# A context ring inside the last key/value head, and Wo loaded under the end of attention

## What is computed

```
def _L0_xattn_ref(latents, context, Wq, Wk, Wv, Wo, q_norm_w, k_norm_w):
    kv = jnp.concatenate([context, latents], axis=1)          # 1857 rows per batch
    q, k, v = latents @ Wq, kv @ Wk, kv @ Wv                  # 32 query heads, 8 key/value heads, 128 wide
    q, k = rms_norm(q, q_norm_w), rms_norm(k, k_norm_w)
    probs = softmax(q @ k.T / sqrt(128)) ; out = probs @ v
    return out @ Wo
x = x + tanh(g_xattn[0]) * _L0_xattn_ref(_layernorm(x), ctx_4096, Wq, Wk, Wv, Wo, q_norm_w, k_norm_w)
x = x + tanh(g_ffn[0]) * _L0_ffn_ref(_layernorm(x), c1_w, c2_w, w1, w2t)   # one row of each 32 chosen
```

## Time and profile before

| | |
|---|---|
| median of 3 runs | 3181.91 us (3180.02 to 3183.23) |
| the profiled execution | 3184.63 us, its span 3182.8 us, mean granted TensorE clock 0.962 |
| busy, share of the span | TensorE 93%, VectorE 78%, ScalarE 64%, GpSimd 44% |
| `prepare` | to about 242 us |
| `attend` | to about 2671 us |
| `project` | its matmuls from 2704 to 2910 us |
| `ffn` | to the end |

### The profile page before, as it was taken

One profiled execution on the slowest core, in us unless ns is written; L12 is line 12 of the kernel. 1 busy time (PEld: TensorE's weight loads), 2 busy tenths in 40 slices (PEclk: granted clock), 3 DMA queues, 4 the chain that ended last, 5 costly groups with the idle time before them and its releaser, 6 DMA issues. The chain is left out here.

```text
span 3182.8 us, 50915 instructions
## 1 busy us (share of the span) xinstructions
PE 2958.6 (93%) x14138; PEld 2398.5 (75%) x14138; DVE 2480.4 (78%) x3285; ACT 2045.6 (64%) x2899; POOL 1386.7 (44%) x791
## 2 busy tenths in 40 slices
PE   7996999999799999997999999899999993887899
PEld 6774888888578888875788888678888872775677
DVE  7773888888858888895888888958888895534765
ACT  3442787888758888884788788758888883211211
POOL 2330455566526655554455656526655554000000
PEclk9997999999999999998999999999999996998899
DMA  7873111121211112122111121211112112856200
GB/s 253 277 217 108 38 39 37 38 41 37 75 38 29 44 37 39 33 60 59 37 34 43 33 34 45 78 37 29 44 36 40 33 24 81 255 159 187 84 30 20
DMA packets 251492, 227.79 MB, mean 72 GB/s; under 512 B 45780, under 2 KB 193236, under 8 KB 250344
## 3 DMA queue, kind: packets, MB, share of 16 engines
q1 hardware_dynamic: 246600, 213.19, 24.5%
q0 software_dynamic: 2176, 8.39, 0.7%
q10 hardware_dynamic: 2592, 4.72, 0.5%
HBM read 156.92 MB, written 69.34 MB: 71 GB/s over the span
## 5 line engine op out<-in xcount | busy, mean ns | idle before, releaser
L877 POOL TENSOR_TENSOR att_sm<-att_sm,att_sc 128x1024 f32<-128x1024 f32 (+1 forms) x384 | 853.8, 2224 | 596.3 <-DVE att_pr L833 594.9
L691 PE MATMUL att_ppv<-att_pr,att_V 128*128 128x512 f32 (+1 forms) x2880 | 866.8, 411 | 27.6 <-DVE att_pr L833 27.1
L671 PE MATMUL att_pqk<-att_q,att_kT 128*128 128x512 f32 (+1 forms) x2880 | 835.5, 400 | 11.3 <-ACT att_sc L760 10.9
L632 PE MATMUL att_pkv<-att_ctxT,att_wkv 128*128 128x512 f32 (+1 forms) x3072 | 761.5, 378 | 5.1 <-DVE att_ctxT L807 4.8
L760 ACT ACTIVATE att_sc<-att_pqk,att_rk 128x512 f32<-128x512 f32 (+1 forms) x960 | 661.6, 690 | 157.0 <-PE att_pqk L671 134.5
L833 DVE TENSOR_TENSOR att_pr<-att_sc,att_pr 128x1024 fp32r<-128x1024 f32 (+1 forms) x512 | 642.0, 1254 | 34.4 <-ACT att_pr L771 21.3
L632 PEld LDWEIGHTS att_pkv<-att_ctxT,att_wkv 128*128 128x128 f32 x3072 | 562.4, 190 | 125.1 <-issue 5.3
L691 PEld LDWEIGHTS att_ppv<-att_pr,att_V 128*128 128x128 f32 (+1 forms) x2880 | 529.3, 193 | 146.5 <-DVE att_pr L833 40.7
L671 PEld LDWEIGHTS att_pqk<-att_q,att_kT 128*128 128x128 f32 (+1 forms) x2880 | 520.5, 185 | 140.3 <-ACT att_sc L760 20.6
L827 DVE TENSOR_TENSOR att_sc<-att_sc,att_pmax 128x1024 f32<-128x1024 f32 (+1 forms) x512 | 585.0, 1142 | 46.0 <-PE att_pmax L640 44.9
L771 ACT CAST att_pr<-att_sc 128x1024 fp32r<-128x1024 f32 (+1 forms) x512 | 511.4, 999 | 109.8 <-PE att_ppv L691 101.6
(11 more groups left out here) (129 smaller groups left out, 2620.3 us busy)
## 6 DMA issues: line engine op xcount, KB each, us to landing
q_scr<-pre_qT SPq DMA_DIRECT2D x128, 256.0 KB, 3.6
att_wkv<-kv_scr SPq DMA_DIRECT2D x64, 512.0 KB, 4.2
att_q<-q_scr SPq DMA_DIRECT2D x64, 512.0 KB, 4.1
o_scr<-att_oraw SPq DMA_DIRECT2D x64, 256.0 KB, 2.0
out_oraw<-o_scr SPq DMA_DIRECT2D x64, 256.0 KB, 4.8
out_rdb<-rd_scr SPq DMA_DIRECT2D x64, 256.0 KB, 5.1
att_sc<-in_ctx SPq DMA_DIRECT2D x16, 768.0 KB, 7.2
pre_wq_raw<-in_L_xattn_Wq SPq DMA_DIRECT2D x8, 1024.0 KB, 6.8
```

The lines of the kernel that those rows point to most:

```text
L632: mm = pe.matmul(bank, wkv[:, which, wp, t], ctxT[:, xp, t, a:z], start=(i == 0), stop=(i == len(terms) - 1))
L671: mm = pe.matmul(pqk[0:m, (h * NT + t) % 2], kT[:, kp, t * P:t * P + m], q[:, qp, h], start=(i == 0), stop=(i == 2))
L691: mm = pe.matmul(ppv[:], V[0:m, vp, t], pr[0:m, pp, (t // 2) % NP, t % 2], start=(t == 0 and i == 0), stop=(t == NT - 1 and i == 2))
L877: pool.tensor_tensor(sm[0:m, 0:w], sm[0:m, 0:w], sc[0:m, h, i:i + w], ALU.add).then_inc(sum_ok, w)
```

## The change

It has two parts and a new table.

**The ring.** The context rows no longer go into `sc`. A buffer `xr` has four slots of one tile each, loaded one tile at a time from ScalarE's DMA queue. The 13 tiles and the load of the latents are placed in the last head's own round (`LAST_SWAP`), each as soon as the V projection of the old batch has read its columns of `ctxT`; the next head's early steps are in that round too. `BOUNDARY` and `FIRST` between batches are gone: the first head of a batch runs the `MIDDLE` list. The tiles use the bank `pred`, which the transposes "mt" and "dt" use as well, so that every user of that bank waits for the one before it. At the very start (`START`) the tiles ("xt0") use three banks.

**The handover.** `handover` gives the two stages shared semaphores and buffers that lie on `ctxT`, on the ring and on the first half's scores. All 8 chunks of Wo (1 MB each) are loaded from SyncE's queue in the last round, after the last V chunk ("ldwo"). The first four units' outputs and three units' inverse sums are loaded in `TAIL` ("ldo"), after the last store of the output. `project` is rewritten with a placed order of its own: units flow from batch to batch, four buffers for the inverse sums instead of two, and each unit's load waits for the low part of the unit four before it.

**The table.** `TILE`, `END`, `CHUNK` and `LOADS` have new values.

```diff
+def handover(nc, ctx, d, Wo):
+    with ExitStack() as first:
+        sb = tools(nc, first, "share")[0]
+        heads = sb("wo", [P, 2 * KT * KVP])
+        tail = sb("wo_tail", [P, WC, D])
+        scores = sb("o_rd", [P, NT * 512])
...
+        ctxT = sb("ctxT", [P, 2, KT, KVP], F32R)
+        xr = sb("xr", [P, XS, D])
+        sc = [sb("sc0", [P, NT, HALF]), sb("sc1", [P, NT, HALF])]
...
-        TILE = dict(copy=0.29, pv=24.4, sub=19.5, exp=21.0, hi=21.6, lo=22.3, sum=23.6, max=1.18)
+        TILE = dict(copy=0.19, pv=24.4, sub=19.4, exp=21.0, hi=21.6, lo=22.4, sum=25.2, max=0.98)
...
-                   dt=(24.37, 24.37),
+                   dt=(23.67, 24.07),
...
-                 dict(k=(0.1, 0.34, 0.62), v=(20.0, 22.44, 22.62), khi=0.64, klo=0.57, kn=4.23, var=4.74, pow=7.34, vhi=21.84, vt=23.7, vthi=23.06, vtlo=22.84))
+                 dict(k=(-0.26, 0.0, 0.32), v=(22.3, 22.84, 22.92), khi=0.24, klo=0.47, kn=3.94, var=6.74, pow=12.84, vhi=21.64, vt=23.6, vthi=23.16, vtlo=23.44))
...
+        for i in range(CT):
+            at = max(at + 1.15, FREE[(S + min(i * P + P, L) - 1) // 512])
+            at = next((z + 0.7 for a, z in HELD if a - 1.1 < at < z + 0.7), at)
+            context += [(at, "xt", 0, i), (at + 0.3, "xhi", 0, i), (at + 0.6, "xlo", 0, i)]
+            ring += [(context[3 * (i - XS)][0] + 0.4 if i >= XS else -0.5 + 0.1 * i, "ldx", 0, i)]
...
+        swap = context + [(max(FREE[0], 0.1), "ldlat", 0, 0)] + ring
...
-        BOUNDARY = window((-1, -UT, late), (0, -UT, in_boundary), (0, 0, context), (0, UT - 3.33, start_early))
-        TAIL = window((-1, -UT, late))
+        handed = [(max(CHUNK[NC - 1]["v"]) + 0.5 + 0.01 * i, "ldwo", 0, i) for i in range(d["HEADS"] // WC)]
+        LAST_ONE = window((-1, -UT, late), (0, 0, own), (0, 0, handed))
+        LAST_SWAP = window((-1, -UT, late), (0, 0, own), (0, 0, swap), (1, UT, early))
+        TAIL = window((-1, -UT, late), (-1, -UT, [(NT + TILE["sum"] + NT - 0.7 + 0.01 * i, "ldo", 0, i) for i in range(SL)]))
...
+        BANK.update({(what, i): 2 for what, n in (("xt", CT), ("mt", NH), ("dt", NH)) for i in range(n)})
...
+            run(0, START, [], xb=0, fresh=0)
+            run(0, FIRST, [(0, START)], xb=0, fresh=0)
+            with eng.Fori(0, B - 1) as b:
+                with eng.Fori(1, KVH - 1) as r:
+                    run(b * KVH + r, MIDDLE, [(1, MIDDLE)], head=r)
+                run(b * KVH + (KVH - 1), LAST_SWAP, [(1, MIDDLE)], xb=b + 1, head=-1, fresh=1)
+                run(b * KVH + KVH, MIDDLE, [(1, LAST_SWAP)], xb=b + 1, fresh=0)
...
+                    if what == "ldx":
+                        act.wait_ge(xt_ps, AHEAD + xb * CT + max(t + 1 - XS, 0))
...
+                        act.dma_start(xr[0:w, t % XS], ctx_4096[bass.ds(xb, 1), t * P:t * P + w]
...
+        steps = [(v - 2.0, "mul", v) for v in range(NV)] + [(v - 1.6, "hi", v) for v in range(NV)]
+        steps += [(v - 1.3, "lo", v) for v in range(NV)] + [(v, "mm", v) for v in range(NV)]
+        steps += [(v - 4.1, "load", v) for v in range(NV)] + [(1.6 + t, "x", t) for t in range(BT)]
...
+        first = [(2 * (c // 2) + (-2.5, -1.5)[c % 2] + 0.8 * (c > 1), "whi", c) for c in range(NW)]
+        first += [(2 * (c // 2) + (-1.9, -1.2)[c % 2] + 0.8 * (c > 1), "wlo", c) for c in range(NW)]
```

More of the change, by code:

```diff
@@ L55, in program @@
     prepare(nc, dims, scratch, x, Wq, Wk, Wv, q_norm_w, k_norm_w)
-    attend(nc, dims, scratch, ctx_4096)
-    project(nc, dims, scratch, x, Wo, g_xattn)
+    with ExitStack() as ctx:
+        shared = handover(nc, ctx, dims, Wo)
+        attend(nc, dims, scratch, ctx_4096, shared)
+        project(nc, dims, scratch, x, g_xattn, shared)
     ffn(nc, dims, scratch, g_ffn, c1_w, c2_w, w1, w2t, out)
@@ L518, in rounds, with run @@
         def rounds(eng, step):
[L520 to L522 removed]
+            def run(n, steps_of, earlier, xb=None, head=0, fresh=None):
+                seen = [(dn - back, *u) for back, w in earlier for dn, *u in uses(w)]
                 for dn, what, h, t in steps_of:
[L524 to L528 removed]
@@ L530, in batch @@
-            def batch(b, loads_of_next):
-                n = b * KVH
-                run(n, FIRST, [(0, BOUNDARY)], xb=b, fresh=True)
+                    if user(what, h, t):
+                        step(n + dn, what, h, t, before=bank_before(seen, *user(what, h, t)), dn=dn, xb=xb, fresh=fresh)
+                        seen.append((dn, *user(what, h, t)))
+                    else:
+                        step(n + dn, what, h, t, xb=xb, dn=dn, head=head)
+            run(0, START, [], xb=0, fresh=0)
@@ L545, in grouped @@
+            run(B * KVH, TAIL, [(1, LAST_ONE)])
+        handed_sems = shared["o_in"] + shared["x_in"] + shared["x2_out"]
+        handed_sems += [shared[n] for n in ("whi_ok", "wlo_ok", "on_ok", "ohi_ok", "olo_ok", "o_ps", "x2_ok")]
         def grouped(n, h, g):
@@ L580, in _, with step @@
             def _(sp):
-                def step(n, what, h, t, before=None, dn=0, last=False, xb=None, head=0, fresh=False):
+                def step(n, what, h, t, before=None, dn=0, xb=None, head=0, fresh=None):
                     if what in ("ldwk", "ldwv"):
@@ L695, in step @@
                         pe.wait_ge(fold_ok, AHEAD + u + 1)
[L696 to L699 removed]
+                        wait_for_bank(n, dn, before, xb)
                         for c in range(4):
```

362 lines of the change are left out of this document (185 added, 177 removed).

## The result

The changed kernel takes **3078.93 us** (median of 4 runs, 3078.22 to 3080.34) against 3182.08 for the one before (4 runs, 3180.02 to 3183.23): ratio 0.9677, 95% interval 0.966 to 0.9694. That is 103 us faster, where 136 were forecast, and 4 us above the range. Its profiled execution took 3079.33 us, with a span of 3077.2 and a mean granted clock of 0.977. So 30.2 us are to be found between the forecast's sum of 3049.1 and 3079.3.

The account below looks back on a forecast made before the run. TensorE's work was taken to bound ordinary rounds (69.7 us), with 122.3 us lost between batches. The sum 3184.6 - 90 - 43.5 - 4 + 2 = 3049.1, with the runs' median 2.7 lower, gave 3046 us; range 3026 to 3075.

Parts of the forecast that it names:

- the swap rounds: The rounds at a batch boundary that hold the context tiles: forecast as one round of 80.4 us, 10.7 extra each boundary.
- first reduction: VectorE's first reduction of a head's first half, after the kernel's start: forecast 4 us sooner.
- start: Kernel's beginning: four single tiles first in their own queue, transposed some 5 us sooner; -4 us in all (-9 to +3).
- The table: Ordinary rounds of attention: new order can't go below 69.7 us, only get waits; +2 us over 28 rounds (-1 to +10).
- dt: Transposes on TensorE that wait for the fold in an ordinary round: taken as the tightest wait, slack 0.8 us.
- Ordinary rounds stall: Rival: slack at "dt" and the shared bank fails, TensorE waits 0.5 us each half; 28 us, 3074; chance 0.1.
- The ring: Last head's round at batch boundaries: 13 tiles add 5.7 us work and 5 us stall; gain 90 us (69 to 105).
- Between batches: Attention's batch boundaries: 43.3, 43.1 and 35.9 us lost, together 122.3, mostly waiting and slow clock.
- no stretch of low clock: Sign of being right: a boundary round of 75 to 88 us with TensorE's clock never low.
- The handover: Attention to `project`: TensorE starts at about 2685 instead of 2704.18, `project` ends at 2866.5; -43.5 us (36 to 50).
- Wo hides: End of attention: Wo's 8 MB, issued some 50 us earlier, are landed by then; the opposite rival, 3065, had chance 0.08.
- Locked out: Rival: in boundary rounds VectorE's low parts meet GpSimd's sums, 1.3 us more each, VectorE needs 89 us; 3073; chance 0.1.

Follow-up runs that it names:

- the late loads: Changed kernel, but with Wo and project's first inputs loaded by SyncE at the start of project, in one queue: 3106.02 us, 0.9769 of the kernel before.

## Why the prediction was wrong, step by step

Forecast and profiled execution differ by 30.2 us. Term by term, us against the forecast:

| step | forecast | measured | difference |
|---|---|---|---|
| ordinary rounds: wait for the copy | +2 in all | 31 waits, 20.6 | +18.6 |
| ordinary rounds: TensorE's own work | 69.67 | 70.45 - 0.67 = 69.78, 28 times | +3 |
| jump of the batch loop | 0 | 4.9 and 4.0 over a round of 70.45 | +8.9 |
| the swap rounds | 3 x 10.7 | 3 x (4.1 + 4.0) | -7.7 |
| first reduction | -4 | 322.38 to 320.40, -2 | +2 |
| last reciprocal to first matmul | 13.9 | 24.3 | +10.4 |
| `project`'s matmuls, with the slow start | 181.5 | 179.0 | -2.5 |
| `ffn` | 272.9 | 270.5 | -2.4 |

They add to 30.3. In `project` three matmuls take 0.69 us once the clock is full, and the forecast took 0.70. The last row is noise: `ffn` is between 270 and 274 us in all these profiles. The first reduction too comes anywhere from 315 to 321 us in kernels with the same start, so that of the **start** no more can be said than that it lost nothing: the first tile is transposed at 256.11 and not at 263.10, 7 us sooner where 5 were forecast, but only 2 of them are left at the first reduction.

- **The table** is the step that failed. "It can only get waits. The tightest one is 'dt'" looked at one wait and its slack. That one held, with more room than the 0.8 us worked out: the fold ended at 578.61 and TensorE's four transposes start without a wait at 581.72. The copy of the output, whose place had hardly moved (23.6 to 23.8), was no candidate, because TensorE had waited for it only once before, 0.2 us. What changed was the cover on TensorE: the matmuls between two products. The end of +10 that I gave this term was no bound at all.
- **The rival "Ordinary rounds stall"** had the size (28 us) and the sign, but at "dt" and the shared bank. Its chance was 0.1, and the run with the table alone has the wait without the shared bank.
- **The ring** was right, and better than forecast. The tiles' work is 73.17 + 72.82 - 2 x 69.74 = 6.5 us a boundary (5.7 forecast), and TensorE's waits for the tiles' low parts are 1.7 us where I took 5. No low clock in either swap round.
- **Between batches** the forecast had no term for the way back of the loop: it took all 122.3 us between batches as lost to the old order, and gave none of it to the jump. What it cost is 8.9 us, in two rounds, with the low clock behind it. So "no stretch of low clock" was right in the swap rounds and wrong in the round after. The rows of before held a sign of it: two boundaries lost 43 us and the last one, which no jump back follows, 35.9. Right after the first two, ScalarE stops twice without a wait that the trace names (2.5 and 5.5 us, then 2.4 and 5.8), and TensorE waits 4.2 and 4.6 us for it; after the third the largest such stop is 0.9. The kernel before at the first:

```profile
906.42 1.27 ACT L760 ACTIVATE att_sc<-att_pqk,att_rk 128x512 f32<-128x512 f32 x2 [5.47 <-issue]
```
```profile
907.16 1.65 PE L671 MATMUL att_pqk<-att_q,att_kT 128*128 128x512 f32 x3 [4.24 <-ACT att_sc L760]
```

  That this is the same jump fits its place in the code and the run with the loop written out, but no run of the kernel before was made without the loop.
- **The handover** was right up to the barrier and wrong by one instruction: "then the first unit: 5.5" left out that ScalarE does the tanh first. With the tanh away, the very same sum was measured: 13.8 against 13.9.
- **Wo hides**: right. The first cast waits for the tanh, never for Wo, and the late loads cost 27 us. The one unbroken run of `project` came as said, 179.0 us.
- **"Locked out"** did not happen. VectorE's low parts took 1255 ns on average in the swap rounds and 1287 in ordinary ones; only at the tail, where the earlier trace rows had it, one still took 2.56 us (at 2590.18):

```profile
L895 DVE TENSOR_TENSOR att_pr<-att_sc,att_pr 128x1024 fp32r<-128x1024 f32 x28 | 35.1, 1255 | 6.2 <-ACT att_pr L833 5.9
```

Two of the three misses, copy and tanh, taken out give 3050.36 us, within 0.2% of the forecast; but that is partly luck, since the jump (+9) and the ring's smaller stalls (-8) cancel in it.

## What to carry to other kernels

When an order is changed, a wait that cost nothing before is the one to look at: for each operation that frees a buffer, ask what stands in front of it in its own engine's queue, and what work on the waiting engine lies between. A new hand-over between stages is as late as the first instruction of each engine in the new stage, so read what that instruction needs, however small. And when a term is summed up as "lost between two stages", ask what each part of it was before crediting the change with all of it: here a boundary that was 7 us shorter than its neighbours pointed at the loop's jump, and a wait of 9.2 us for a store of 2 KB at the end of attention pointed at a store that is slow to land, with which the loads put behind it landed too.

## What the runs showed of the hardware

- A store of 2 KB in 512 pieces of four bytes took 10.1 to 11.0 us to land at the end of attention, and 7.8 to 10.1 over the 64 of the kernel before. A load issued right behind it landed with it, from the same queue (9.5 us) and from another one (9.1); issued after it had landed, the same load took 2.7. During most of one such store the DMA share was 0.00.
- The jump back of a loop whose body is three rounds' lists long stopped TensorE for 1.7 and 2.0 us, and its clock was then 0.50 in one stretch of 4 us; in all a round lost 4 to 5 us. With the loop written out the stop was gone. The loop over one round's list, with 346 matmuls in it, showed none.
- The sixth of the 14 loads, moved ahead of the last output store, held SyncE's queue for 8.09, 8.18 and 7.74 us in the three runs that had them there, where the five before it took 0.6 each; behind that store the sixth took 0.6 as well. Its cause was not tried.
